# First attention: two half-seen key blocks merged into one, and a new order of the items

## The chip, the cores and the metric

The kernel runs on one core of a Trainium2 chip. The metric is the time of one execution on the device in microseconds (us); lower is better. TensorE (PE) multiplies matrices, VectorE (DVE), ScalarE (ACT) and GpSimd (POOL) work elementwise, SyncE (SP) issues the loads. Each engine runs its own instructions in order; semaphores are all that ties the engines together.

## The reference, cut to what matters

The program computes two transformer layers of different kinds on x of 2 x 512 x 512, in fp32. The change lies in the first layer's attention:

```
q = rope(x @ wq)   # 32 heads of 128         k, v = rope(x @ wk), x @ wv   # 8 heads; 4 q heads share one
scores  = q . k / sqrt(128)
allowed = (j <= i) & (j > i - 128)           # 512 positions
attn    = softmax(where(allowed, scores, -big));   out = (attn @ v) @ wo
```

With positions in blocks of 128, a block of queries sees two blocks of keys: its own where j <= i, and the block before where j > i. In each row the seen columns of the one are just the unseen columns of the other: 128 keys in all. The first query block has no block before.

## The kernel before, in words

For each of 8 key heads and 2 batches (a *half*, `half = 2 * n + b`) the kernel projects K, V and four Q heads, turned so that features lie on partitions, and handles four *slots*, one for each query block `qb` of 128 rows, with its four query heads side by side. Every fp32 product is made of three matmuls of numbers split into a high part (rounded to fp32r) and the low rest, so each operand is written twice: `_hi` by ACT or VectorE, `_lo` by VectorE or POOL (`mm3`, L2032).

A slot goes through these steps. `scores` (PE, L2155) puts the products of four heads with 256 keys into banks 0 and 1. `mask` (DVE, L1538) adds the window to each head's scores by one fused instruction, which also gives the row's maximum. `exps` (ACT, L1070) makes the exponentials of each head and their sums. `normalise` (DVE, L1550) takes reciprocals and multiplies four heads at once, 1024 columns. `transposes` (PE, L2167) turns eight blocks of 128 x 128 into banks 2 and 3. `weights_high` (ACT, L1079) and `weights_low` (DVE, L1560) split them, an instruction per bank. `sum_values` (PE, L2175) multiplies both key blocks with V: six matmuls of 512 columns. `out_high`, `out_low`, `project_out`, `gate_attention` (DVE, L1588) and `add_attention` (POOL, L711) turn the result into an update of x. Slot 0 of a half has one key block, so half of each step.

While the slots of a half run, the next half's projections are made in banks 6 and 7, which alternate: a projection waits until the one before the last has been taken out of its bank (`proj_free`). Q and K leave it by `evacuate` (DVE, L1517; three rope products), `rope_add` (POOL, L693), `rope_high` (ACT) and `rope_low` (POOL, L699); V is copied, transposed back by PE (`Vt`), and split.

The order of all this is written out by hand, in one `kv_head` per engine; each half of the loop has the same items. The loop covers 15 halves; the last half is interleaved with the start of the layer's second part, and the first is preceded by a prologue. `split_weights`, `weights_high0`, `split_wo` and `out_weights_high` prepare the next head's weights, in every other half.

Of the kernel before, what the change touches and what calls it, by code (L numbers as in the profile page):

```python
# [6 lines left out]
F32R = mybir.dt.float32r  # L7
I32 = mybir.dt.int32
# [6 lines left out]
P = 128  # L15
# [51 lines left out]
def adaln_two_layers(nc, a, out):  # L67
# [8 lines left out]
    with ctx:  # L76
# [14 lines left out]
        cT = sb("cT", [P, 2, B, KT])  # L91
        silu_e = sb("silu_e", [P, 2, B, KT])
        silu_d = sb("silu_d", [P, 2, B, KT])
# [29 lines left out]
        v_hi = sb0("v_hi", [P, B, TB, HD], F32R)  # L123
        v_lo = sb0("v_lo", [P, B, TB, HD], F32R)
# [26 lines left out]
        gate_f0 = sb0("gate_f0", [P, B, D])  # L151
        qT_hi, qT_lo = (bq0_hi, bq1_hi), (bq0_lo, bq1_lo)
# [169 lines left out]
        kr_mm, kr_hi_done, kr_split, zeroed = sem("kr_mm"), sem("kr_hi_done"), sem("kr_split"), sem("zeroed")  # L322
# [91 lines left out]
        def _(sp):  # L414
# [44 lines left out]
            sp.dma_start(window[:], a["window_mask"]).then_inc(rope_loaded, 16)  # L459
            load_q(0)  # L460
# [220 lines left out]
        def _(pool):  # L681
# [73 lines left out]
            def kv_head(n, last):  # L755
                for b in range(1 if last else B):
                    half = 2 * n + b
                    split = b == 0 and not last
                    if b == 0:
                        split_wo(n)  # L760
                    if not (isinstance(n, int) and n == 0 and b == 0):
                        add_attention(4 * half - 1, TB * (1 - b) + 3)
# [4 lines left out]
                    rope(half + 1, "Q1", 1 - b)  # L767
                    rope(half + 1, "Q2", 1 - b)
                    add_attention(4 * half, TB * b)
                    rope(half + 1, "Q3", 1 - b)  # L770
                    add_attention(4 * half + 1, TB * b + 1)
                    if split:
                        split_weights(n + 1, (1,))
                    if not last:
                        rope_add(half + 2, "K", b)
                    add_attention(4 * half + 2, TB * b + 2)
                    if not last:
                        rope_low(half + 2, "K", b)
                    if split:
                        split_weights(n + 1, (2,))  # L780
                    if split:
                        split_weights(n + 1, (3, 4, 5))

# [29 lines left out]
            add_attention(4 * LAST - 1, 3)  # L813
            add_attention(4 * LAST, TB)
            add_attention(4 * LAST + 1, TB + 1)
            add_attention(4 * LAST + 2, TB + 2)
# [193 lines left out]
        def _(act):  # L1010
# [55 lines left out]
            def v_high(half, b):  # L1066
                act.wait_ge(proj_done, TURNS * half + TURN["Vt"] + 1)
                act.activation(v_hi[:, b].rearrange("p t d -> p (t d)"), bank[6 + (b + TURN["Vt"]) % 2][:], ACT.Copy).then_inc(v_hi_done, 1)

            def exps(slot, qb):  # L1070
                i = qb % 2
                c = slice(P, 2 * P) if qb == 0 else slice(0, 2 * P)
                act.wait_ge(masked0, slot + 1)
                for h in range(GQ):
                    e = act.activation(probs[:, i, h, c], probs[:, i, h, c], ACT.Exp, bias=nmax[:, i, h:h + 1], scale=-1.0,  # L1075
                                       accum_out=den[:, i, h:h + 1])
# [25 lines left out]
            def kv_head(n, last):  # L1102
                for b in range(1 if last else B):
# [4 lines left out]
                    weights_high(slot, 0)  # L1108
                    out_high(slot)
# [4 lines left out]
                    exps(slot + 1, 1)  # L1114
                    rope_high(half + 1, "Q0", nb)
                    weights_high(slot + 1, 1)
                    v_high(half + 1, nb)
                    exps(slot + 2, 2)
                    rope_high(half + 1, "Q1", nb)
                    out_high(slot + 1)  # L1120
                    weights_high(slot + 2, 2)
                    exps(slot + 3, 3)
                    rope_high(half + 1, "Q2", nb)
                    out_high(slot + 2)
# [1656 lines left out]
```

## Time and profile before

| | |
|---|---|
| median of 3 runs | 2203.28 us (2202.14 to 2205.8) |
| profiled execution, its own time | 2204.66 us |
| its span | 2202.8 us |
| busy over the span: PE, DVE, ACT, POOL | 98%, 77%, 66%, 56% |
| granted TensorE clock, mean | 0.995 |

The first attention takes the stretch from about 60 to 730 us of the span. A busy share is that of an engine's own instructions, waits left out; matmuls overlap, so PE's is no measure of its peak. "Idle before" in a list is the time that an engine waited ahead of the instructions of a group, and the name behind the arrow is what released it. In a list of instructions by time, one that is blocked after it has started shows as longer.

### The profile page before, as it was taken

To read this page: it belongs to the slowest core of one execution; us is meant where nothing else is said; L and a number is where in the kernel's file an instruction comes from. 1 tells how busy PE (TensorE), PEld (TensorE's weight loads), DVE (VectorE), ACT (ScalarE), POOL (GpSimd) and SP (SyncE) were. 2 spreads that over 40 slices of the span, in tenths; PEclk is the share of its full clock that TensorE was granted. 3 is DMA by queue.
4 is the path that set the end of the run, shared out by engine and by line. 5 is a ranking of instruction groups with operands and counts; after the bars stand their busy time and mean duration, and the time that the engine had idled before them with its cause. 6 is when DMAs were issued, how large, how long until landed. Compare 5 with 4: busy or idle time off the path is not lost.

```text
span 2202.8 us, 41666 instructions
## 1 busy us (share of the span) xinstructions
PE 2151.4 (98%) x11084; PEld 1653.8 (75%) x11084; DVE 1700.4 (77%) x3415; ACT 1460.7 (66%) x2868; POOL 1232.4 (56%) x1091
## 2 busy tenths in 40 slices
PE   7999999999999999999999999999999999999988
PEld 5888888888887657777777777777777777777756
DVE  6777777777777668888888888888888877788865
ACT  3444444445444668888888888888888877777742
POOL 5656655665653446666666666666666620455334
PEclk9999999999999999999999999999999999999999
DMA  7011010010004142111111111111111111433341
GB/s 245 20 48 30 19 48 29 19 48 29 19 10 125 40 176 82 43 48 49 46 49 42 49 46 48 42 49 46 49 42 48 47 49 42 124 92 111 87 126 39
DMA packets 125422, 132.20 MB, mean 60 GB/s; under 512 B 33205, under 2 KB 75733, under 8 KB 125348
## 3 DMA queue, kind: packets, MB, share of 16 engines
q1 hardware_dynamic: 121508, 118.70, 18.1%
q0 software_dynamic: 3840, 12.59, 1.9%
q8 instruction: 37, 0.61, 0.1%
q14 instruction: 37, 0.30, 0.0%
HBM read 101.46 MB, written 29.10 MB: 59 GB/s over the span
## 4 chain that ended last, share of the span: by engine, by line
PE 92%; DVE 4%; ACT 1%; SPq 1%; issue 1%; POOL 0%; DMA 0%; DVEq 0%; ACTq 0%; POOLq 0%
PE bank L2464 12%; PE bank L2451 11%; PE bank L2471 11%; PE bank L2036 9%; PE bank L2038 9%; PE bank L2037 9%; PE bank L2492 6%; PE bank L2383 5%; PE bank L2382 5%; PE bank L2381 5%; PE bank L2489 2%; PE bank L2172 2%; DVE rope_b L1535 1%; DVE rope_b L1536 1%; DVE rope_a L1534 1%
## 5 line engine op out<-in xcount | busy, mean ns | idle before, releaser
L1817 DVE TENSOR_REDUCE mcol<-bank 128x1 fp32r<-128x512 f32 x1024 | 693.9, 689 | 221.6 <-PE bank L2451 211.2
L2464 PE MATMUL bank<-q,k 128*128 128x512 f32 x1024 | 418.8, 409 | 0.1
L2451 PE MATMUL bank<-km,q 128*128 128x512 f32 x1024 | 405.7, 397 | 2.9 <-DVE mcol L1817 1.6
L2471 PE MATMUL bank<-q,k 128*128 128x512 f32 x1024 | 406.2, 397 | 0.0
L2451 PEld LDWEIGHTS bank<-km,q 128*128 128x128 f32 x1024 | 316.2, 309 | 52.3 <-DVE mcol L1817 4.2
L1329 ACT ACTIVATE pT<-bank 128x512 f32<-128x512 f32 x512 | 284.5, 600 | 81.6 <-PE bank L2471 77.8
L1329 ACT ACTIVATE x<-bank 128x512 f32<-128x512 f32 x512 | 284.6, 600 | 80.8 <-PE bank L2471 77.0
L2464 PEld LDWEIGHTS bank<-q,k 128*128 128x128 f32 x1024 | 192.2, 188 | 127.0 <-ACT x L1329 44.3
L2471 PEld LDWEIGHTS bank<-q,k 128*128 128x128 f32 x1024 | 192.3, 188 | 32.4
L2383 PE MATMUL bank<-hT_hi,wr_lo 128*128 128x512 f32 x512 | 202.9, 396 | 0.0
L2381 PE MATMUL bank<-hT_hi,wr_hi 128*128 128x512 f32 x512 | 200.7, 392 | 1.6 <-DVE k L1690 1.6
L2382 PE MATMUL bank<-hT_lo,wr_hi 128*128 128x512 f32 x512 | 201.6, 394 | 0.0
L705 POOL TENSOR_TENSOR bq_lo<-rope_a,bq_hi 128x512 fp32r<-128x512 f32 x64 | 105.1, 1644 | 144.1 <-ACT bq_hi L1064 144.1
L849 POOL CAST pH<-x 128x512 f16<-128x512 f32 x96 | 58.7, 612 | 194.0 <-ACT x L1329 194.0
L2036 PE MATMUL bank<-hT_hi,w_hi 128*128 128x512 f32 x376 | 153.5, 408 | 6.9 <-DVE rope_b L1536 6.9
L1075 ACT ACTIVATE probs<-probs,nmax 128x256 f32<-128x256 f32 (+1 forms) x256 | 120.1, 475 | 57.6 <-DVE nmax L1546 57.6
L801 POOL TENSOR_TENSOR wr_lo<-wst,wr_hi 128x512 fp32r<-128x512 f32 x64 | 83.0, 1297 | 129.3 <-DVE wr_hi L1683 129.2
L697 POOL TENSOR_TENSOR rope_a<-rope_a,rope_b 128x512 f32<-128x512 f32 x80 | 111.6, 1394 | 67.3 <-DVE rope_b L1536 67.2
L1082 ACT ACTIVATE pT_hi<-bank 128x512 fp32r<-128x512 f32 x112 | 61.7, 596 | 131.3 <-PE bank L2172 131.3
L2038 PE MATMUL bank<-hT_hi,w_lo 128*128 128x512 f32 x376 | 147.2, 392 | 0.0
L2037 PE MATMUL bank<-hT_lo,w_hi 128*128 128x512 f32 x376 | 146.7, 390 | 0.0
L849 POOL CAST pH<-pT 128x512 f16<-128x512 f32 x96 | 58.5, 610 | 131.0 <-ACT pT L1329 131.0
(348 smaller groups left out, 5045.6 us busy)
## 6 DMA issues: line engine op xcount, KB each, us to landing
wst<-in_L_attn_Wq_rope SPq DMA_DIRECT2D x64, 256.0 KB, 3.0
o_d<-ost SPq DMA_DIRECT2D x504, 32.0 KB, 1.8
st_q<-in_L_attn_wq SPq DMA_DIRECT2D x8, 1024.0 KB, 7.4
st_wo<-in_L_attn_wo SPq DMA_DIRECT2D x8, 1024.0 KB, 5.2
km<-kc_d SPq DMA_DIRECT2D x256, 32.0 KB
q<-qc_d SPq DMA_DIRECT2D x256, 32.0 KB
k<-kc_d SPq DMA_DIRECT2D x256, 32.0 KB
wm<-in_L_wmod SPq DMA_DIRECT2D x6, 1024.0 KB, 9.3
```

What stands on the lines that cost most here:

```text
L1329: act.activation(PT[k % 2][:, s], bank[s % 4][:], ACT.Exp, scale=float((HD1 + ROPE) ** -0.5)).then_inc(exp1, 1)
L1817: dve.tensor_reduce(mcol[:, k % 2, i % 4, i // 4:i // 4 + 1], bank[4 + i % 2][:], AX.X, ALU.max, negate=True)\
L2036: pe.matmul(ps, lh_, rh, start=(i == 0), stop=False)
L2037: pe.matmul(ps, lh_, rl, start=False, stop=False)
L2038: e = pe.matmul(ps, ll, rh, start=False, stop=(i == n - 1))
L2381: pe.matmul(bank[6][:], wr_hi[:, par, kk], hT_hi[:, kk, at], start=(kk == 0), stop=False)
L2382: pe.matmul(bank[6][:], wr_hi[:, par, kk], hT_lo[:, kk, at], start=False, stop=False)
L2383: e = pe.matmul(bank[6][:], wr_lo[:, par, kk], hT_hi[:, kk, at], start=False, stop=(kk == KT - 1))
L2451: pe.matmul(bank[4 + i % 2][:], q2[:, k % 4, h, i % 4:S:4], km[:, b, h], start=True, stop=True).then_inc(max_mm, 1)
L2464: pe.matmul(bank[s % 4][:], k1[:, k % 2, t], q1[:, k % 4, h], start=True, stop=False)
L2471: pe.matmul(bank[s % 4][:], k2[:, k % 2, h, t], q2[:, k % 4, h], start=False, stop=True).then_inc(scores1, 1)
L2492: e = pe.matmul(rows(s), vp[:, k % 2, kb, h], PT[k % 2][:, s], start=(s < 4), stop=(s >= 4))
```

## The change

In slots 1 to 3 the two half-seen blocks are merged into one of 128 columns. `mask` copies the scores of the block before to SBUF, overwrites those of the own block where j <= i by a predicated copy, takes one maximum over the four heads' rows and scales it. `exps`, `normalise`, `transposes` and `weights_high` then handle 128 columns per head. As the merged weights m belong to two value blocks, the sum is made as m times V of the block before, plus (m where own) times the difference of V between the blocks: `weights_low` makes the masked high part, and a new POOL instruction, `own_weights`, the masked low part. `dv_hi` and `dv_lo` hold the difference, made with `Vt` and two new items, `dv_high` (ACT) and `dv_low` (DVE). A 0/1 constant `own` is loaded. Semaphore counts follow (`masked0` goes up by 5 per slot, `pT_split` by 2), and the items of `kv_head` are reordered on all four engines.

```diff
             def exps(slot, qb):
                 i = qb % 2
-                c = slice(P, 2 * P) if qb == 0 else slice(0, 2 * P)
-                act.wait_ge(masked0, slot + 1)
+                c = slice(P, 2 * P) if qb == 0 else slice(0, P)
+                act.wait_ge(masked0, 5 * slot + 5)
...
             def weights_high(slot, qb):
                 act.wait_ge(trans0, slot + 1)
-                for kb in range(1 if qb == 0 else 0, 2):
-                    e = act.activation(pT_hi[:, kb], bank[2 + kb][:], ACT.Copy)
-                e.then_inc(pT_hi_done, 1)
+                act.activation(pT_hi[:, 0], bank[2 + qb % 2][:], ACT.Copy).then_inc(pT_hi_done, 1)
...
+            def own_weights(slot):
+                heads = lambda v: v.rearrange("p (h q) -> p h q", h=GQ)
+                mine = own[:].unsqueeze(1).broadcast_to([P, GQ, P])
+                pool.wait_ge(pT_split, 2 * slot + 1)
+                pool.tensor_tensor(heads(pT_lo[:, 1]), heads(pT_lo[:, 0].bitcast(F32)), mine, ALU.mult).then_inc(pT_split, 1)
...
                 if name == "Vt":
-                    dve.wait_ge(v_hi_done, half + 1)
-                    dve.tensor_tensor(v_lo[:, b]..., ps[:], v_hi[:, b]..., ALU.subtract).then_inc(proj_free, 1)
+                    later = vT[:, 0:3 * P]
+                    dve.wait_ge(v_hi_done, 2 * half + 1)
+                    dve.tensor_tensor(flat(v_lo[:, b]), ps[:, 0:3 * P], flat(v_hi[:, b]).bitcast(F32), ALU.subtract)
+                    dve.tensor_tensor(later, ps[:, P:4 * P], flat(v_hi[:, b]).bitcast(F32), ALU.subtract).then_inc(kv_split, 1)
+                    dve.wait_ge(kv_split, 2 * half + 1)
+                    dve.tensor_tensor(later, later, flat(v_lo[:, b]).bitcast(F32), ALU.subtract).then_inc(proj_free, 1)
...
+            def dv_low(half, b):
+                dve.wait_ge(v_hi_done, 2 * half + 2)
+                dve.tensor_tensor(dv_lo[:]..., vT[:, 0:3 * P], dv_hi[:]..., ALU.subtract).then_inc(kv_split, 1)
...
             def mask(slot, qb):
...
+                block = lambda j, kb: bank[j][:].rearrange("p (h k) -> p h k", h=2)[:, :, kb * P:(kb + 1) * P]
+                seen = window[:, 0:P].bitcast(U32).unsqueeze(1).broadcast_to([P, 2, P])
+                for j in range(2):
+                    dve.tensor_copy(probs[:, i, 2 * j:2 * j + 2, 0:P], block(j, 0)).then_inc(masked0, 1)
+                dve.wait_ge(masked0, 5 * slot + 2)
+                dve.sem_inc(spare, 1)
+                for j in range(2):
+                    e = dve.copy_predicated(probs[:, i, 2 * j:2 * j + 2, 0:P], seen, block(j, 1))
                 e.then_inc(masked0, 1)
+                dve.wait_ge(masked0, 5 * slot + 3)
+                dve.tensor_reduce(nmax[:, i], probs[:, i, :, 0:P], AX.X, ALU.max, negate=True).then_inc(masked0, 1)
+                dve.wait_ge(masked0, 5 * slot + 4)
+                dve.tensor_scalar(nmax[:, i], nmax[:, i], scale, None, ALU.mult).then_inc(masked0, 1)
...
             def weights_low(slot, qb):
                 dve.wait_ge(pT_hi_done, slot + 1)
-                for kb in range(1 if qb == 0 else 0, 2):
-                    e = dve.tensor_tensor(pT_lo[:, kb], bank[2 + kb][:], pT_hi[:, kb].bitcast(F32), ALU.subtract)
-                e.then_inc(pT_split, 1)
+                if qb > 0:
+                    dve.tensor_tensor(heads(pT_hi[:, 1]), heads(bank[2 + qb % 2][:]), own..., ALU.mult)
+                dve.tensor_tensor(pT_lo[:, 0], bank[2 + qb % 2][:], pT_hi[:, 0].bitcast(F32), ALU.subtract)\
+                   .then_inc(pT_split, 2 if qb == 0 else 1)
```

The order of a half's items on VectorE and TensorE (`s` the half's first slot, primes the next half):

```
DVE before: gate(s-1) mask(s+1) weights_low(s) Q0' Q1' out_low(s) normalise(s+1) mask(s+2) weights_low(s+1) Vt'
            gate(s) normalise(s+2) out_low(s+1) Q2' mask(s+3) weights_low(s+2) normalise(s+3) Q3' out_low(s+2)
            gate(s+1) weights_low(s+3) gate(s+2) K'' mask(s+4) out_low(s+3) V'' normalise(s+4)
DVE after:  gate(s-1) mask(s+1) weights_low(s) Q0' normalise(s+1) Q1' mask(s+2) out_low(s) weights_low(s+1) Vt'
            gate(s) normalise(s+2) Q2' out_low(s+1) weights_low(s+2) mask(s+3) Q3' gate(s+1) normalise(s+3)
            out_low(s+2) K'' weights_low(s+3) mask(s+4) out_low(s+3) gate(s+2) dv_low' V'' normalise(s+4)
PE before:  scores(s+1) T(s) Q0' sum(s) Q1' Vt' scores(s+2) Q2' T(s+1) out(s) sum(s+1) scores(s+3) T(s+2) Q3'
            out(s+1) sum(s+2) T(s+3) K'' out(s+2) sum(s+3) scores(s+4) V'' out(s+3)
PE after:   scores(s+1) T(s) Q0' sum(s) Q1' scores(s+2) Vt' T(s+1) Q2' out(s) scores(s+3) sum(s+1) T(s+2) Q3'
            out(s+1) sum(s+2) K'' T(s+3) out(s+2) scores(s+4) sum(s+3) V'' out(s+3)
```

On POOL, `own_weights(s+1)` comes behind Q1's rope items, `own_weights(s+2)` behind Q2's, `own_weights(s+3)` ahead of K's; `add_attention(s)` moves ahead of Q2's, and the `add_attention` of the slot before moves ahead of `split_wo`. On ACT, `weights_high(s+2)` moves ahead of `out_high(s+1)`, and two of the next head's weight splits move ahead of `exps(s+2)`.

## Rows read from the trace of the kernel before

**Rows 1.** Stretches: us, busy PE PEld DVE ACT POOL (x), clock, DMA share, GB/s.
```profile
342.90:384.97 42.07, 41.58 (x222) 35.43 (x222) 31.28 (x73) 19.29 (x54) 25.59 (x20) 1.00 0.12 37
```
**Rows 2.** Waits, 130 to 690 us: us in total, times, longest.
```profile
PE bank L2036 <- DVE rope_b L1536: 6.3, 13, 0.5
```
**Rows 3.** Chain of waits, one half: start, us, what.
```profile
357.51 0.44 PE bank L2172 x4
...
365.64 0.69 DVE rope_b L1536
...
369.46 0.87 PE bank L2172 x8
```
**Rows 4.** Instructions by time, TensorE, same half: start, us.
```profile
355.91 0.28 PE L2036 MATMUL bank<-kT_hi,bq_hi 128*128 128x256 f32 x1
...
360.53 0.39 PE L2036 MATMUL bank<-pT_hi,v_hi 128*128 128x512 f32 x1
...
361.21 0.39 PE L2036 MATMUL bank<-hT_hi,w_hi 128*128 128x512 f32 x1
...
363.94 0.60 PE L2145 MATMUL bank<-ident,vT 128*128 128x128 f32 x4
...
365.68 0.28 PE L2038 MATMUL bank<-kT_hi,bq_lo 128*128 128x256 f32 x1
366.45 0.49 PE L2036 MATMUL bank<-hT_hi,w_hi 128*128 128x512 f32 x1 [0.49 <-DVE rope_b L1536]
366.78 0.39 PE L2037 MATMUL bank<-hT_lo,w_hi 128*128 128x512 f32 x1
```
**Rows 5.** Instructions by time, VectorE, same half.
```profile
357.70 0.42 DVE L1546 CUSTOM_DVE_ANT_0 probs<-bank,window 128x256 f32<-128x256 f32 x1 [0.90 <-PE bank L2038]
...
358.06 0.42 DVE L1546 CUSTOM_DVE_ANT_0 probs<-bank,window 128x256 f32<-128x256 f32 x1
...
358.40 0.42 DVE L1546 CUSTOM_DVE_ANT_0 probs<-bank,window 128x256 f32<-128x256 f32 x1
...
366.35 0.69 DVE L1568 TENSOR_TENSOR oT_lo<-bank,oT_hi 128x512 fp32r<-128x512 f32 x1
366.96 0.17 DVE L1554 RECIPROCAL rden<-den 128x4 f32<-128x4 f32 x1
367.16 1.61 DVE L1557 TENSOR_TENSOR probs<-probs,rden 128x1024 f32<-128x1024 f32 x1
```
**Rows 6.** Groups by line and shape, whole span; one line's own instructions (L1481).
```profile
L1817 DVE TENSOR_REDUCE mcol<-bank 128x1 fp32r<-128x512 f32 x1024 | 693.9, 689 | 221.6 <-PE bank L2451 211.2
L1528 DVE COPY vT<-bank 128x512 f32<-128x512 f32 x16 | 11.0, 690 | 14.9 <-PE bank L2038 14.9
L1546 DVE CUSTOM_DVE_ANT_0 probs<-bank,window 128x128 f32<-128x128 f32 x64 | 14.8, 287 | 3.5 <-PE bank L2038 2.2 <-issue 0.6
L1481 DVE TENSOR_SCALAR var_eps<-mean_var x8: 169/170/540, 10.9 to 2147.3; 128x4 f32<-128x4 f32 x8
```
**Rows 7.** Instructions by time, VectorE and POOL: products alone and beside POOL.
```profile
354.21 0.69 DVE L1557 TENSOR_TENSOR probs<-probs,rden 128x512 f32<-128x512 f32 x1
374.14 1.22 DVE L1557 TENSOR_TENSOR probs<-probs,rden 128x1024 f32<-128x1024 f32 x1
396.27 1.69 DVE L1557 TENSOR_TENSOR probs<-probs,rden 128x512 f32<-128x512 f32 x1
366.40 1.29 POOL L697 TENSOR_TENSOR rope_a<-rope_a,rope_b 128x512 f32<-128x512 f32 x1 [0.17 <-DVE rope_b L1536]
374.49 2.02 POOL L705 TENSOR_TENSOR bq_lo<-rope_a,bq_hi 128x512 fp32r<-128x512 f32 x1 [6.80 <-ACT bq_hi L1064]
396.12 1.29 POOL L705 TENSOR_TENSOR kT_lo<-rope_a,kT_hi 128x512 fp32r<-128x512 f32 x1 [0.74 <-ACT kT_hi L1064]
```
**Rows 8.** Chain of waits, prologue.
```profile
40.20 0.69 DVE rope_a L1534
...
51.30 1.27 POOL rope_a L697
```

More of the change, by code:

```diff
@@ L151, in adaln_two_layers @@
         gate_f0 = sb0("gate_f0", [P, B, D])
+        with ExitStack() as first:
+            sbs = sbuf_in(first)
+            cT = sbs("cT", [P, 2, B, KT])
+            silu_e = sbs("silu_e", [P, 2, B, KT])
+            silu_d = sbs("silu_d", [P, 2, B, KT])
+        dv_lo = sb0("dv_lo", [P, TB - 1, HD], F32R)
         qT_hi, qT_lo = (bq0_hi, bq1_hi), (bq0_lo, bq1_lo)
@@ L773, in kv_head @@
                         split_weights(n + 1, (1,))
+                    own_weights(4 * half + 3)
                     if not last:
@@ L782, in kv_head @@
                         split_weights(n + 1, (3, 4, 5))
+                    if not last:
+                        rope_low(half + 2, "K", b)
             kv_head(0, False)
@@ L1135, in kv_head @@
                         weights_high0(n + 1, 5)
+                    out_high(slot + 2)
+                    rope_high(half + 1, "Q3", nb)
+                    weights_high(slot + 3, 3)
                     if not last:
                         rope_high(half + 2, "K", b)
+                    out_high(slot + 3)
+                    dv_high(half + 1, nb)
+                    exps(slot + 4, 0)
             def merged_turned(t):
@@ L1527, in evacuate @@
                 if name == "V":
+                    wait(dve, kv_split, 2 * half)
                     dve.tensor_copy(vT[:], ps[:]).then_inc(proj_free, 1)
@@ L2157, in scores @@
                     pe.wait_ge(rope_split, 5 * half + 5)
-                wait(pe, masked0, slot)
+                wait(pe, masked0, 5 * slot if qb == 1 else 5 * slot - 2)
                 c = slice(P, 2 * P) if qb == 0 else slice(0, 2 * P)
@@ L2179, in sum_values @@
                 wait(pe, oT_split, slot)
-                mm3(bank[4][:], [(v_hi[:, b, qb - 1 + kb], v_lo[:, b, qb - 1 + kb], pT_hi[:, kb], pT_lo[:, kb])
-                                 for kb in range(1 if qb == 0 else 0, 2)], pv0)
+                at = max(qb - 1, 0)
+                pe.matmul(bank[4][:], v_hi[:, b, at], pT_hi[:, 0], start=True, stop=False)
+                pe.matmul(bank[4][:], v_hi[:, b, at], pT_lo[:, 0], start=False, stop=False)
+                e = pe.matmul(bank[4][:], v_lo[:, b, at], pT_hi[:, 0], start=False, stop=(qb == 0))
+                if qb > 0:
+                    pe.wait_ge(pT_split, 2 * slot + 2)
+                    pe.matmul(bank[4][:], dv_hi[:, at], pT_hi[:, 1], start=False, stop=False)
+                    pe.matmul(bank[4][:], dv_hi[:, at], pT_lo[:, 1], start=False, stop=False)
+                    e = pe.matmul(bank[4][:], dv_lo[:, at], pT_hi[:, 1], start=False, stop=True)
+                e.then_inc(pv0, 1)
             def project_out(slot, n):
@@ L2239, in kv_head @@
                     project(half + 1, "Q1", nb, n + b)
+                    scores(slot + 2, half, b, 2)
                     project(half + 1, "Vt", nb, n + b)
-                    scores(slot + 2, half, b, 2)
+                    transposes(slot + 1, 1)
                     project(half + 1, "Q2", nb, n + b)
-                    transposes(slot + 1, 1)
                     project_out(slot, n)
+                    scores(slot + 3, half, b, 3)
                     sum_values(slot + 1, half, b, 1)
-                    scores(slot + 3, half, b, 3)
                     transposes(slot + 2, 2)
@@ L2250, in kv_head @@
                     sum_values(slot + 2, half, b, 2)
-                    transposes(slot + 3, 3)
                     if not last:
                         project(half + 2, "K", b, n + 1)
+                    transposes(slot + 3, 3)
                     project_out(slot + 2, n)
+                    scores(slot + 4, half + 1, nb, 0)
                     sum_values(slot + 3, half, b, 3)
+                    if not last:
+                        project(half + 2, "V", b, n + 1)
                     if isinstance(n, int) and n == 0 and b == 0:
                         pe.wait_ge(gate_ready, 1)
-                    scores(slot + 4, half + 1, nb, 0)
-                    if not last:
-                        project(half + 2, "V", b, n + 1)
                     project_out(slot + 3, n)
```

119 lines of the change are left out of this document (66 added, 53 removed).

## The prediction, made before the changed kernel was run

> **What bounds the kernel now.** I read the table of busy time by stretch first, with the granted clock beside it: the middle of the first attention, cut at its own period [rows 1]. A half (one key head, one batch) takes 42.07 us; in it TensorE is busy 41.6 us at the full clock (1.00), VectorE 31.3, ACT 19.3, POOL 25.6. So TensorE sets the pace, and VectorE has some 10 us of idle time. Then the list of waits of the stage [rows 2]: what TensorE itself waits for is a rope product of VectorE, 6.3 us in 13 waits. The chain of waits of one half shows where that sits: after the second set of scores the third query projection waits for the rope products of the second, because both use one PSUM bank [rows 3]. The order of TensorE's instructions says what such a wait costs [rows 4]: the last scores matmul starts at 365.68 and the next would start 0.12 later, at 365.80; it starts at 366.45, and its successor follows after 0.33 instead of the usual 0.23. So 0.65 + 0.10 = 0.75 us per half. All starts below are counted from the half's first scores, 355.91 [rows 4]. Without that wait a half would take 42.07 - 0.75 = 41.32 us.
>
> **What goes from TensorE.** Four transposes take 0.44 us of the chain, eight take 0.87 [rows 3]. In three slots of four, eight become four: 3 x 0.435 = 1.31 us per half. The matmuls of the weights with the values stay six (three on the block before, three on the difference). So 41.32 - 1.31 = 40.01 us is the floor of a half, 2.06 below now; there are 15 full halves, so at most 31 us.
>
> **What VectorE gets.** It is the engine that has to follow, so each piece is priced.
> - The mask now is four fused instructions of 256 columns, 0.34 us apart (358.06 to 358.40), so 4 x 0.34 = 1.37 us [rows 5]. In its place: two copies of 256 columns from PSUM, two predicated copies, one reduce of 512, one multiplication of four numbers, with three waits for its own results between. A 512-column read of PSUM takes 0.69 [rows 6] and the 256-column one 0.42, with the next 0.34 later [rows 5]: a pair ends after 0.34 + 0.42, and 0.04 passes at a wait for one's own result, as between reciprocal (0.17) and product [rows 5]. Copies 0.80, predicated copies 0.80, reduce 0.69 + 0.04 (a reduce of 512 columns takes 0.69, from PSUM [rows 6]; from SBUF I take the same), multiplication 0.1: 2.43 us. No row shows a predicated copy. From below it is bounded by the 128-column instruction, 0.29, from above by the 512-column one, 0.69 [rows 6]; I take 0.42, that of equal width. The mask so lies between 2.2 and 3.0 us.
> - The product with the reciprocals is 512 columns instead of 1024: 0.69 instead of 1.22 when undisturbed [rows 7]. The low weights stay two instructions of 0.61. The values' low part becomes three dependent instructions (0.47 + 0.56 + 0.03 + 0.56 = 1.6 in place of 0.61) and the difference's low part adds 0.5.
> - Per half: 3 x (2.43 - 1.37) - 3 x 0.5 + 1.0 + 0.5 = +3.2 us. That fits the 10 us of idle time as a sum; whether it fits in the order is the question.
>
> **The port.** A product of two SBUF tensors waits for POOL. The 512-column one takes 0.69 alone and 1.69 when POOL has begun an instruction 0.15 us earlier, ending 0.55 after POOL's; and POOL takes 2.02 in place of 1.29 when the product came first [rows 7]. Right behind rope products POOL wins: it starts 0.08 after their end (366.32 to 366.40), the product 0.2 behind the reciprocal that lies between [rows 3, 5, 7]. The four-number multiplication takes 0.17 and once 0.54 [rows 6], so it too seems to wait.
> The Trainium skill's page "SBUF — State Buffer", section "Who interferes with whom", says the same of products and of a multiplication on SBUF data (whoever begins first blocks the other for its whole instruction), and adds that a reduce never takes part; the trace has no reduce from SBUF beside POOL. By that rule the sum stays as below; were the reduce to wait as well, each mask could grow by up to a POOL instruction, 1.29, which is more of the slower rival.
>
> **The order, followed through one half.** TensorE's pieces are read from [rows 4]: a projection of twelve matmuls 2.73 us (361.21 to 363.94), also the output's; three matmuls of the values 0.68 (360.53 to 361.21), so six 1.37; scores 1.42 with the transposes of V ahead of them 1.86 (363.94 to 365.80); four transposes 0.44. VectorE's: rope products three times 0.70, a two-input instruction on PSUM 0.61 to the next [rows 5].
> 1. Scores end, mask from 1.79 (where it starts now [rows 4, 5]) to 4.22; low weights of the slot before end 4.91, TensorE gets them at 5.04 (0.13 later, as from 366.32 to 366.45 [rows 3, 4]). It wants them at 4.62: late by 0.42.
> 2. Rope products of Q0 4.83 to 6.94. The product of the slot, now ahead of Q1's, waits for POOL's rope sum (7.02 to 8.31) and ends at 8.86. Q1's projection, itself moved by step 1, is ready at 8.85, so the port costs nothing here. Rope products of Q1 to 10.95; Q2 starts at 11.08. Without waits it would be 10.34 (Vt and the transposes are ahead of it). Cost of steps 1 and 2 together 0.74 + 0.10 = 0.85 us. So the old wait stays, since everything from the mask on is one VectorE chain.
> 3. Next mask to 13.4, and the low output, now behind it, to 14.1; the output projection, due 2.83 after Q2's start at 13.91, starts at 14.23: 0.32 + 0.10 = 0.42 us.
> 4. TensorE: output projection to 17.06, scores to 18.48, six matmuls to 19.85, where it wants the next product. VectorE's low weights and the values' part end by 17.4, the gate (behind the output projection) at 18.0, the product behind `own_weights` at about 19.3: in time. `own_weights` of this slot runs on POOL from about 17.2 to 18.5 and is wanted at 19.2.
> 5. Rope products of Q2 to 21.5, low output at 22.3 (it waits for ACT), low weights 23.5, mask 26.0 plus 0.3 for the small multiplication behind `own_weights`, rope products of Q3 28.35, gate 28.96, product behind POOL's rope sum 30.25. TensorE wants it at 19.85 + 0.44 + 2.73 + 2.73 + 1.37 + 2.73 = 29.85, gets it at 30.38: 0.53 + 0.10 = 0.6 us (rounded).
> 6. The rest of the half: key rope, low weights by 35, first mask, difference's low part and `own_weights` come before their readers.
>
> The waits come to 0.85 + 0.42 + 0.60 = 1.87 us, so a half takes 40.01 + 1.87 = 41.88: 0.19 us less than now, 15 x 0.19 = 2.8 us.
> POOL's three `own_weights` are 3 x 1.29 [rows 7], on an engine with 16 us idle per half; behind them queue the adds of x and the rope sums, which have microseconds. ACT loses a copy and half of the exponentials' columns per slot, in an engine idle for more than half of the time [rows 1]. The DMA of the new constant is 64 KB behind loads that TensorE doesn't wait for.
>
> **Before and after the loop.** In the prologue the chain runs through VectorE from 40.20 to 51.2 and then through POOL [rows 8]. The longer values' part (+1.0) and the difference's low part (+0.6) stand in it: +1.6 us. In the last half three sets of transposes go (-1.3), and the waits for VectorE's longer masks take some 0.5 back: -0.8.
>
> **Sum.** The profiled execution took 2204.66 us (span 2202.8). -2.8 + 1.6 - 0.8 = -2.0: 2202.7 us. It lies 1.4 above the median of the runs shown, 2203.28; from the median the forecast is 2201.3, say 2201. About 0.2% (4.4 us) is what a measurement can tell from no change.
>
> **The rivals.**
> - *VectorE keeps up* (25%). If the mask costs 2.0 us instead of 2.43, steps 1 to 3 lose 0.9 us and step 5 about 0.45 more, to about 0.5 of waits: 15 x -1.5 = -23, about 2181; with no wait at all 2203 - 31 + 1 = 2173. For it: 10 us idle per half, and new waits sit at a few tenths. Against: every step of the new mask waits for the one before.
> - *The predicated copy costs double* (20%; the other side). At 0.69 each, the mask is 0.54 longer; it stands three times in the chain that TensorE waits for, and the first time it counts more because Q1 moves too, 3.25 x 0.54 = 1.75 per half: 15 x 1.75 - 2 = +24, about 2227. It decides from about 0.06 us more per copy on. For it: nothing shows this instruction. Against: equal width costs equal time in all others [rows 5, 6].
> - *`own_weights` comes late* (10%). The second three matmuls wait for POOL, which serves a rope sum and a rope remainder first. In slot 2 it has 0.2 us to spare by my count; late by 0.6 in two of three slots (2 x 0.5 + 0.2 lost) it is +1.2 per half, 15 x 1.2 - 2 = +16, about 2219.
> - *The change saves no TensorE time* because transposes hide behind weight loads: 2203 + 1 plus the waits, above 2215; the 0.44 to 0.87 step of rows 3 speaks against it, I give it nothing of its own.
>
> **How the numbers follow.** The forecast 45%, with its own range 2194 to 2209 (a tenth of a microsecond per mask is 0.33 per half, 5 us in all); the rivals 25, 20 and 10. The range of 8 in 10 is 2180 to 2224: it takes in most of the first and a good part of the second. Faster by over 0.2%: 25 + 12 = 37%. Within 0.2%: 28%. Slower: 30 + 5 = 35%.
>
> **What would show it.** After: transposes 256 instead of 448; four rows of 0.44 us in the chain; mask steps 0.42, 0.42, 0.42, 0.42, 0.69 and under 0.2, 2.4 us together; a half of 41.9 us, with TensorE's idle time at Q2 (0.75), at the first output projection (0.3) and before the transposes of slot 3 (0.5), released by VectorE; VectorE's idle time per half down from 10 to some 7 us. It is wrong if a predicated copy is not 0.42, if TensorE's waits name POOL, or if a half is outside 41.4 to 42.4.

## The result, and the profile after

The changed kernel takes 2256.07 us (median of 4 runs, 2255.61 to 2260.36) against 2204.54 us of the kernel before on the same chip (2202.14 to 2205.89): a ratio of 1.0239, 95% interval 1.0222 to 1.0257. The profiled execution took 2256.01 us. The forecast was 2201, with a range of 2180 to 2224: the change costs 51.5 us where 2 us of gain were expected.

The first rows of the page: the span, and each engine's busy time and instructions.
```profile
span 2254.2 us, 41585 instructions
PE 2169.3 (96%) x10892; PEld 1643.4 (73%) x10892; DVE 1794.3 (80%) x3367; ACT 1422.4 (63%) x2836; POOL 1288.2 (57%) x1139
```
Three halves of the changed kernel, the view of [rows 1]: us, busy PE PEld DVE ACT POOL, clock, DMA share, GB/s. The first two belong to batch 0, the third to batch 1.
```profile
242.01:286.99 44.98, 41.71 (x211) 33.92 (x209) 38.44 (x69) 19.77 (x54) 30.57 (x21) 1.00 0.07 23
330.11:377.92 47.81, 44.56 (x210) 36.04 (x209) 38.44 (x69) 19.66 (x54) 30.62 (x21) 0.93 0.06 22
377.92:421.07 43.15, 41.77 (x210) 33.95 (x209) 36.91 (x69) 14.74 (x47) 28.16 (x22) 1.00 0.11 36
```
A half took 42.07 us whatever its batch [rows 1]. Now a half of batch 1 takes 43.1 us (the first 42.9) and one of batch 0 45.0 to 48.3, so the last half starts 44.0 us later than before (736.8 against 692.8 us): 1.5 us from ahead of the loop, 42.5 in its 15 halves (673.8 against 631.3). Look at TensorE's busy time: 41.7 us in the first and the third, but 44.56 in the second, for the same instructions, at a clock of 0.93.

The list of waits, 130 to 690 us, as in [rows 2]:
```profile
ACT probs L1100 <- DVE nmax L1600: 92.0, 37, 4.3
...
PE bank L2236 <- DVE pT_lo L1616: 24.6, 12, 2.9
```
The old wait for the rope products is gone from it. TensorE waits for `weights_low` ahead of the first values of each half, up to 2.9 us (3.4 in the first half, which this window leaves out). VectorE by time there shows why (start, us):
```profile
332.77 0.79 DVE L1595 COPY_PREDICATED probs<-window,bank 128x256 f32<-128x256 uint32 x2
333.59 0.69 DVE L1598 TENSOR_REDUCE nmax<-probs 128x4 f32<-128x512 f32 x1
334.31 2.72 DVE L1600 TENSOR_SCALAR nmax<-nmax 128x4 f32<-128x4 f32 x1
336.95 0.68 DVE L1616 TENSOR_TENSOR pT_lo<-bank,pT_hi 128x512 fp32r<-128x512 f32 x1
```
and GpSimd beside it:
```profile
332.44 4.57 POOL L698 TENSOR_TENSOR wo_lo<-st_wo,wo_hi 128x2048 fp32r<-128x2048 f32 x1
```
The multiplication of four numbers begins at 334.31 and ends at 337.03; GpSimd's `wo_lo` ends at 337.01. The Trainium skill's page "SBUF — State Buffer", section "Who interferes with whom", counts a `tensor_scalar` from on-chip memory to on-chip memory among the instructions that can contend with GpSimd, and says that whichever of the two engines issues second is fully blocked until the other's instruction is over. The trace agrees, with 2.72 us in place of 0.17. It also shows that semaphores are not all that ties the engines together: none stands between these two instructions. In batch-1 halves GpSimd has only instructions of 1.3 us there, and the multiplication takes 1.20 us. All forms of the line together (smallest, median, largest, ns):
```profile
L1600 DVE TENSOR_SCALAR nmax<-nmax x48: 169/170/3368, 67.2 to 754.9; 128x4 f32<-128x4 f32 x48
```
TensorE behind two of these waits, in a half that kept its clock and in one that lost it (from the timeline of its own instructions):
```profile
249.75 0.47 PE L2236 MATMUL bank<-pT_hi,v_hi 128*128 128x512 f32 x1 [2.91 <-DVE pT_lo L1616]
250.06 0.40 PE L2237 MATMUL bank<-pT_lo,v_hi 128*128 128x512 f32 x1
250.29 0.39 PE L2238 MATMUL bank<-pT_hi,v_lo 128*128 128x512 f32 x1
...
337.87 0.76 PE L2236 MATMUL bank<-pT_hi,v_hi 128*128 128x512 f32 x1 [2.91 <-DVE pT_lo L1616]
338.43 0.63 PE L2237 MATMUL bank<-pT_lo,v_hi 128*128 128x512 f32 x1
338.86 0.63 PE L2238 MATMUL bank<-pT_hi,v_lo 128*128 128x512 f32 x1
...
343.55 0.63 PE L2092 MATMUL bank<-hT_lo,w_hi 128*128 128x512 f32 x1
343.98 0.44 PE L2093 MATMUL bank<-hT_hi,w_lo 128*128 128x512 f32 x1
```
The wait is 2.91 us both times. After the first the matmuls follow each other every 0.23 us, the 2.4 GHz level. After the second they come every 0.43 us up to 343.98, the 1.2 GHz level: 13 matmuls take 5.55 us instead of 3.0, so 2.5 us are lost behind a wait of 2.9. The half does not win them back: its first output projection starts 20.0 us after its start, against 17.2 in the half that kept the clock. Two batch-0 halves of eight (45.0 us) kept it. The others lost it, for 3 to 6 us: the first five of those are 1.3 to 2.8 us longer, 8.8 together.

The product with the reciprocals (L1608), the pieces of the mask and one piece of the values' low part (L1553), as groups of the whole span:
```profile
L1608 DVE TENSOR_TENSOR probs<-probs,rden 128x512 f32<-128x512 f32 x64 | 73.2, 1144 | 2.2
L1595 DVE COPY_PREDICATED probs<-window,bank 128x256 f32<-128x256 uint32 x96 | 37.6, 445 | 7.1 <-DVE probs L1591 3.4
L1600 DVE TENSOR_SCALAR nmax<-nmax 128x4 f32<-128x4 f32 x48 | 36.2, 754 | 1.7
L1591 DVE COPY probs<-bank 128x256 f32<-128x256 f32 x96 | 36.1, 418 | 15.8 <-PE bank L2093 15.3
L1598 DVE TENSOR_REDUCE nmax<-probs 128x4 f32<-128x512 f32 x48 | 32.9, 686 | 1.6
L1553 DVE TENSOR_TENSOR vT<-vT,v_lo 128x384 f32<-128x384 f32 x15 | 18.6, 1239 | 0.5
```
Copy, predicated copy and reduce are as forecast (0.42, 0.45, 0.69 us). The mean of 0.754 us for the multiplication is no typical value: its median is 0.17, and the long ones all stand in slot 1. L1553, another product of two on-chip tensors, took 1.24 us where the forecast had 0.56.

### The profile page after: what moved, and what is told of

The parts are those of the page before. It is cut to its first block, busy times and chain, and to the rows that moved or that the text cites. A ratio compares the mean times of both kernels' runs of the same rounds, so it can differ in the third digit from the quotient of the medians.

```text
span 2254.2 us, 41585 instructions
## 1 busy us (share of the span) xinstructions
PE 2169.3 (96%) x10892; PEld 1643.4 (73%) x10892; DVE 1794.3 (80%) x3367; ACT 1422.4 (63%) x2836; POOL 1288.2 (57%) x1139
## 4 chain that ended last, share of the span: by engine, by line
PE 87%; DVE 7%; issue 3%; ACT 1%; POOL 1%; SPq 1%; DMA 0%; DVEq 0%; ACTq 0%; POOLq 0%
PE bank L2527 12%; PE bank L2514 11%; PE bank L2534 10%; PE bank L2091 7%; PE bank L2093 7%; PE bank L2092 7%; PE bank L2555 6%; PE bank L2446 5%; PE bank L2444 5%; PE bank L2445 5%; PE bank L2552 2%; PE bank L2236 1%; PE bank L2227 1%; DVE probs L1591 1%; DVE nmax L1598 1%
## 5 line engine op out<-in xcount | busy, mean ns | idle before, releaser
L1100 ACT ACTIVATE probs<-probs,nmax 128x128 f32<-128x128 f32 x256 | 99.6, 390 | 120.1 <-DVE nmax L1600 116.1
L704 POOL TENSOR_TENSOR rope_a<-rope_a,rope_b 128x512 f32<-128x512 f32 x80 | 103.5, 1294 | 102.8 <-DVE rope_b L1566 102.8
L1106 ACT ACTIVATE pT_hi<-bank 128x512 fp32r<-128x512 f32 x64 | 38.3, 598 | 163.8 <-PE bank L2227 163.8
L712 POOL TENSOR_TENSOR bq_lo<-rope_a,bq_hi 128x512 fp32r<-128x512 f32 x64 | 83.1, 1300 | 83.6 <-ACT bq_hi L1084 83.6
```

## The experiments

All timed against the kernel before, run on the same chip (2205.2 to 2206.5 us). Where "one run" stands there is a single execution, and no interval. A half's length is the time between the first scores of slot 1 in two successive halves, read from TensorE's timeline.

**e1_tables and e1b_recip: the multiplication taken away, or something that cannot be blocked in its place.** The factor 1/sqrt(128) goes into the rope tables (its root in each; `exps` then scales by 1), and the reduce signals in its place. The second kernel has, beyond that, a reciprocal of the four maxima that nobody reads.
```
-    scale = float(HD) ** -0.5
+    scale = 1.0
-    dve.tensor_reduce(nmax...).then_inc(masked0, 1)
-    dve.wait_ge(masked0, 5 * slot + 4)
-    dve.tensor_scalar(nmax[:, i], nmax[:, i], scale, None, ALU.mult).then_inc(masked0, 1)
+    dve.tensor_reduce(nmax...).then_inc(masked0, 2)
+    "rope_cos": cos * HD ** -0.25      (rope_sin likewise)
```

> The changed kernel, with the factor 128^-0.5 of the scores put into the rope tables of q and k (128^-0.25 each), so that the small multiplication of four maxima in the mask is gone; everything else as in the changed kernel. Theory (the small multiplication waits for the SBUF port while POOL works: 2.7 us in every half of batch 0 behind the 4.6 us split of wo, 1.2 in the others): TensorE's wait before the first value matmuls falls from 2.9 and 1.2 us to 0.2 to 0.5 in all halves, TensorE's clock no longer falls in the loop, a half takes 42.0 to 42.4 us instead of 43.15 and 45.0 to 48.3, the time is 2212 to 2218 us. Rival (the chain of five dependent steps in the mask is simply long, the instruction's own 0.17 us is all that goes): 3 x 0.2 x 15 = 9 us, about 2247.

> As the kernel with the factor in the tables, but in place of the multiplication stands a reciprocal of the same four numbers into a spare tile: same place, same wait, same 0.17 us, an instruction that never waited for POOL in the traces so far. Port theory: 0.17 us in all 48 places, and the time within 5 us of the kernel without the instruction (2214 to 2222). Rival (a fifth dependent step costs): within 10 us of the changed kernel, 2246 or more.

Measured: e1_tables 2213.5 us (5 runs; ratio to before 1.0041, 1.0026 to 1.0055), halves 41.6 to 42.0 us (the last of the loop 42.6), TensorE idle 0.25 us ahead of the first values in batch 0 and hardly at all in batch 1. The multiplication of four numbers, three times in each half, was worth 42.6 us (43.3 with each kernel taken against the kernel before of its own chip). e1b_recip 2212.7 us (one run), halves 41.9 to 42.5 (the last 44.2). Its line:
```profile
L1601 DVE RECIPROCAL spare<-nmax x48: 177/178/179, 66.3 to 715.8; 128x4 f32<-128x4 f32 x48
```
A reciprocal of the same size, same place and same operand was never held. So it is the kind of instruction, not its place behind the reduce. Yet e1_tables stays 8 us over the kernel before, though its loop (628.5 us) is as fast as forecast.

**e2_pieces: `wo_lo` of the changed kernel in four instructions of 512 columns.**
```
-    pool.tensor_tensor(wo_lo[:], st_wo[:], wo_hi[:]...).then_inc(wo_split, 1)
+    for h in range(GQ):
+        e = pool.tensor_tensor(wo_lo[:, h], st_wo[:, h], wo_hi[:, h]...)
+    e.then_inc(wo_split, 1)
```

> The changed kernel with POOL's 2048-column split of wo cut into four instructions of 512 columns (4 x 1.3 us). Port theory: the small multiplication waits for one piece at most, so its 2.7 us in halves of batch 0 become 1.3 or less, TensorE's wait 2.9 becomes 1.4 or less, the clock stays up, these halves take 43.2 to 43.6 us instead of 45.0 to 48.3: 2230 to 2238 us. If POOL's pieces kept the port between them (no hand-over), nothing changes: 2256. If the wait has nothing to do with POOL: 2256.

Measured: 2228.0 us (one run), waits of 0.9 us in batch 0 and 1.2 in batch 1, halves 42.9 to 43.2 us (the first 42.1, the last 44.5), clock 0.993 instead of 0.989. The multiplication is held for 0.7 us in batch 0, where it was 2.7. A shorter GpSimd instruction makes a shorter block, and waits of about 1 us left the clock alone. The result is a little below what was expected.

**e3_old_order: merged blocks, order of items as before.** 

> The merged blocks as in the changed kernel, but the items of the loop in the order of the kernel before on all four engines (the new items put in at the first place where their inputs are there). Port theory: the small multiplication stands in the same place against the split of wo, so the 2.7 us wait stays in half of the halves; time within 12 us of 2256. Rival (the new order is what costs): the time comes back to 2200 to 2215.

Measured: 2391.5 us (one run). Both expected times missed by over 120 us; the multiplication was held as in the changed kernel (2.6 us in batch 0, 3.7 in the first half; 1.1 to 1.3 in batch 1). TensorE's list of waits, 130 to 690 us:
```profile
PE bank L2241 <- POOL pT_lo L723: 63.0, 22, 4.0
PE bank L2236 <- DVE pT_lo L1616: 19.8, 10, 2.8
```
So most of TensorE's waiting there is for `own_weights` on GpSimd. The new order is worth 135 us to the merged version; it is no cause of the loss.

**b2_small: the same kind of instruction, alone, in the kernel before.**
```
+    if qb > 0:
+        dve.tensor_scalar(spare4[:], ident[:, 0:GQ], 0.5, None, ALU.mult)
```

> The kernel before plus one multiplication of four numbers per partition that nobody reads (a tile of its own from the first four columns of ident), on VectorE behind each mask of query blocks 1 to 3. Theory 1 (a small tensor_scalar waits for the end of a GpSimd operation on the tensors): wherever it falls inside wo_lo (4.6 us) or w_lo it takes 1 to 4 us, elsewhere 0.17 us, though it depends on nothing; at least 8 of the 48 are longer than 1 us and the total rises by 3 to 25 us. Theory 2 (it was long in the changed kernel only because it depended on the reduction just ahead, or had its own result as operand): 0.17 to 0.2 us in all 48, total within 3 us of the kernel before.

Measured: 2246.7 us (one run), 41 us slower, more than either theory gave. VectorE, then GpSimd:
```profile
422.93 3.62 DVE L1551 TENSOR_SCALAR spare<-ident 128x4 f32<-128x4 f32 x1
426.46 0.68 DVE L1566 TENSOR_TENSOR pT_lo<-bank,pT_hi 128x512 fp32r<-128x512 f32 x1
```
```profile
421.95 4.57 POOL L692 TENSOR_TENSOR wo_lo<-st_wo,wo_hi 128x2048 fp32r<-128x2048 f32 x1 [2.90 <-ACT wo_hi L1101]
```
It depends on nothing and nobody reads it, and it still waits for the end of `wo_lo` (426.52). Batch-0 halves took 45.4 to 47.5 us. So this one instruction reproduces most of the loss without merged blocks or a new order. Not all of the 41 us are its own: its tile of 16 bytes also moved the other tiles, by 32 bytes, and b1_layout below shows what a move can cost (5.5 us in the loop, 11 in all).

**e4_late_max: the changed kernel with reduce and multiplication of slot 1 behind `weights_low`.**
```
     mask(slot + 1, 1)              # copies and predicated copies only
     weights_low(slot, 0)
+    maximum(slot + 1, 1)           # reduce, multiplication
```

> The changed kernel as it is, with its multiplication of the four maxima, but in slot 1 of each half the reduction and the multiplication stand behind weights_low(slot 0). Theory 1 (the long multiplication costs because weights_low and so the first value matmuls are queued behind it): the multiplication still takes about 2 to 2.7 us in batch-0 halves and 1.2 us in batch-1 halves, the TensorE no longer waits 2.9 and 1.2 us before the first value matmuls, the clock does not fall in the loop, and the time comes to 2212 to 2225 us. Theory 2 (whatever is held on VectorE for 2.7 us is paid in full, since exps(slot 1) and the rope products of Q0 come after it): the wait shows up before the second projection or the transposition instead, total 2240 us or more.

Measured: 2245.8 us (one run): the pessimistic theory. Halves 42.4 and 44.1 to 46.2 us (the last 48.0); the multiplication held for 2.3 us in batch 0 and 0.75 in batch 1. TensorE, 130 to 690 us:
```profile
PE bank L2098 <- DVE rope_b L1566: 12.9, 12, 1.4
PE bank L2234 <- DVE probs L1613: 5.8, 10, 0.9
```
Moved behind one reader, the same block hits the next two, as VectorE works through one chain. And the clock falls behind two shorter waits, 2 us apart (two batch-0 halves, of 44.1 and 44.2 us, had the same two waits and kept it):
```profile
428.50 0.66 PE L2234 MATMUL bank<-ident,probs 128*128 128x128 f32 x4 [0.81 <-DVE probs L1613]
430.50 0.49 PE L2098 MATMUL bank<-hT_hi,w_hi 128*128 128x512 f32 x1 [1.35 <-DVE rope_b L1566]
...
431.70 0.63 PE L2099 MATMUL bank<-hT_lo,w_hi 128*128 128x512 f32 x1
432.13 0.63 PE L2100 MATMUL bank<-hT_hi,w_lo 128*128 128x512 f32 x1
```

**b1_layout: the kernel before with the tiles moved, and nothing else.** The change moves cT, silu_e and silu_d (192 bytes) from the front of the memory to its end, and with them every large tile of the first attention.
```
-    cT = sb(...); silu_e = sb(...); silu_d = sb(...)      # ahead of rowsum
+    with ExitStack() as first:                            # behind gate_f0
+        cT = sbs(...); silu_e = sbs(...); silu_d = sbs(...)
```

> The kernel before with one part of the change alone: the tiles cT, silu_e and silu_d stand behind gate_f0 instead of in front of rowsum, so every later tensor of the second attention lies 192 bytes lower in each partition; no instruction is added or removed. In all four kernels profiled with the change, the second attention, where TensorE is busy all the time, took 749.1 to 751.9 us between the 100th and the 400th matmul hT_hi x wr_hi, against 748.0 before. Theory 1 (addresses): this stretch takes 750 to 751 us here too and the total rises by 4 to 8 us. Theory 2 (it is the scatter of executions, or it comes from something else of the change): 748.0 +- 0.5 us and a total within 2 us of the kernel before.

Measured: 2216.7 us (4 runs; ratio 1.0051, 1.0034 to 1.0068): 11 us slower without one instruction changed. Halves 42.47 us, matmuls 100 to 400 of `hT_hi x wr_hi` 750.6 us. In a projection of twelve matmuls, first of it and first instruction behind it:
```profile
366.92 0.39 PE L2038 MATMUL bank<-hT_hi,w_hi 128*128 128x512 f32 x1
...
369.72 0.60 PE L2147 MATMUL bank<-ident,vT 128*128 128x128 f32 x4
```
2.80 us, against 361.21 to 363.94 = 2.73 before [rows 4]. Six projections make 0.4 us per half, the whole of the difference between halves. That is theory 1, with more than it asked for: the loop is 5.5 us longer (636.8 us), and the stretch of the second attention from its first `wr` matmul to its last 6.1 us (1305.5 against 1299.4).

**e6_tables_late: e1_tables with the late maximum.** 

> The changed kernel with the factor in the rope tables (no multiplication of the four maxima) and, in slot 1 of each half, the reduction moved behind weights_low(slot 0): VectorE does the copies, the predicated copies, weights_low, then the maximum. With the factor in the tables alone the TensorE waited 0.25 us before the first value matmuls and a half took 41.6 to 42.0 us. Theory 1 (the queue of VectorE sets that wait): it is gone, the reduction's 0.69 us now delays exps(slot 1), which has over 5 us until its transposition; halves 41.4 to 41.8 us, start of the last half 3 to 5 us earlier than with the tables alone, total 2207 to 2212 us. Theory 2 (the next wait, VectorE's rope products, takes its place): halves unchanged within 0.1 us, total 2211 to 2216 us.

Measured: 2210.1 us (10 runs; 1.0021, 1.0011 to 1.0030). The wait ahead of the values is gone, and rope_b took its place (5.6 us in 13 waits); halves 41.8 and 41.9. The total lies in the range of theory 1, but the halves are within 0.1 us of e1_tables and the next wait took the place of the old one: theory 2.

**e7_aligned, b3_pad128, e8_after_aligned: which places are good.** e7 is e6_tables_late and e8 the changed kernel, both with nmax and den behind dv_lo, which brings the large tiles 64 bytes lower; b3 is the kernel before with an unused tile of 128 bytes ahead of rowsum. The edit of e7 and e8:
```
-    nmax = sb("nmax", [P, 2, GQ]); den = sb("den", [P, 2, GQ])
     dv_lo = sb0("dv_lo", [P, TB - 1, HD], F32R)
+    nmax = sb0("nmax", [P, 2, GQ]); den = sb0("den", [P, 2, GQ])
```

> The kernel with the factor in the tables and the late maximum in slot 1, with nmax and den moved behind dv_lo, so that w_hi, w_lo and all other large tensors lie 64 bytes lower and again at a multiple of 128 bytes from the first tensor, as in the kernel before (in the changed kernel they lie 64 bytes off one). Moving the three small tiles alone, without any change of an instruction, had cost the kernel before 11 us (2216.72 against 2205.66), with 0.2333 us instead of 0.2281 from one projection matmul to the next. Theory 1 (the start of the matmuls' operands against 128 bytes sets it): spacing 0.228 us, halves 41.4 to 41.6 us, stretch of the second attention 748 us, total 2197 to 2202 us, faster than the kernel before. Theory 2 (only the exact place of before is good, or the relation to something else): spacing 0.233, halves 41.8 to 42.0, total 2208 to 2212 us.

> The kernel before with an unused tile of 128 bytes in front of rowsum: everything behind it lies 128 bytes higher, still at multiples of 128 bytes. Theory 1 (128 bytes): spacing 0.228 us, halves 42.07 us, total within 2 us of the kernel before. Theory 2 (any other place than that of before costs, or a multiple of 256 or 512 bytes is wanted): spacing 0.233 us, halves 42.47 us, total 2214 to 2218 us.

> The changed kernel with all its instructions, nmax and den moved behind dv_lo as above. It prices the tiles' places within the change. Theory 1 (128 bytes): 2243 to 2247 us, that is 9 to 13 us of the change's 51 us come from the places of the tiles and 38 to 42 from the multiplication; batch-1 halves 42.7 to 42.8 us instead of 43.14. Theory 2: 2254 to 2258 us, halves as in the changed kernel.

Measured: b3_pad128 2215.4 us (4 runs; 1.0045, 1.0030 to 1.0060), a projection in 2.80 us, halves 42.4: against the theory, 128 bytes are not enough. e7_aligned 2208.0 us (11 runs; 1.0007, 0.9998 to 1.0016), e8_after_aligned 2249.7 us (2 runs, 2246.5 and 2252.9), both with projections of 2.72 us where the clock was full. In e8 a half of batch 1 takes 43.0 us, 0.1 less than in the changed kernel. For e7 the spacing is that of theory 1, the total that of theory 2; of e8's two runs one lies in the range of theory 1, the other between the two. e7_aligned:
```profile
365.39 0.39 PE L2096 MATMUL bank<-hT_hi,w_hi 128*128 128x512 f32 x1
...
368.11 0.28 PE L2096 MATMUL bank<-kT_hi,bq_hi 128*128 128x256 f32 x1
```
```profile
PE bank L2096 <- DVE rope_b L1566: 6.7, 13, 0.6
PE bank L2232 <- DVE probs L1611: 2.8, 2, 2.5
PE bank L2096 <- DVE oT_lo L1624: 1.3, 6, 0.2
```
VectorE's product in slot 1, beside GpSimd's rope sum, comes late for the first of them:
```profile
367.25 1.67 DVE L1611 TENSOR_TENSOR probs<-probs,rden 128x512 f32<-128x512 f32 x1
```

**e9_no_collision: e7_aligned with GpSimd kept off the product in slot 1.**
```
     split_wo(n)                      # heads 0 and 1 only
+    pool.wait_ge(probs0, 4 * half + 2)
     rope_add(half + 1, "Q0", 1 - b)
+    if b == 0: split_wo_rest(n)      # heads 2 and 3
```

> The kernel e7_aligned (factor in the tables, late maximum in slot 1, tiles at the places modulo 256 bytes of before) with GpSimd's work in slot 1 arranged around VectorE's product of weights and reciprocals: GpSimd begins the addition of Q0's rope only when that product is done (one wait more), and wo_lo is made in two halves, one ahead of it and one behind. In e7_aligned the projection matmuls were 0.005 us faster each than without the alignment (0.36 us of 72 per half), but the halves stayed at 41.75 and 41.87 us: TensorE waits 0.47 to 0.57 us for Q1's rope_b ahead of the projection of Q2, and VectorE comes late there because its product took 1.67 us beside GpSimd's addition (0.99 us in slot 2, where GpSimd was idle). Theory 1 (this collision took the gain): the product takes 1.0 to 1.1 us, the wait for rope_b falls to 0 to 0.1 us, halves 41.3 to 41.5 us, total 2200 to 2204 us, faster than the kernel before. Theory 2 (VectorE's queue is late for other reasons, or the next wait replaces it): halves 41.7 to 41.9 us, total 2206 to 2210 us.

Measured: 2201.05 us (median of 12 runs, one of which took 5392.5 us; 2200.94 without it, 0.9975 of the kernel before, 0.9966 to 0.9985). This version beats both kernels, by 5 us and by 55. The half that answers to [rows 1], then VectorE's product:
```profile
352.14:393.48 41.34, 41.23 (x211) 34.03 (x210) 34.26 (x66) 14.68 (x47) 28.10 (x22) 1.00 0.12 38
```
```profile
359.31 0.69 DVE L1617 TENSOR_TENSOR probs<-probs,rden 128x512 f32<-128x512 f32 x1
```
The product took 1.67 us at this place in e7 beside GpSimd's rope sum, and takes 0.69 alone; TensorE's wait for rope_b has left the list. Halves are 41.33 (batch 1) and 41.59 us (batch 0, where the product of slot 2 is now held, for 1.74 us instead of 0.99). The total is that of theory 1, and so are the halves of batch 1; it had the others 0.1 us shorter.

TensorE in that half, at the transposes of slot 1:
```profile
362.04 0.60 PE L2238 MATMUL bank<-ident,probs 128*128 128x128 f32 x4
362.68 0.49 PE L2102 MATMUL bank<-hT_hi,w_hi 128*128 128x512 f32 x1
```
From the start of the transposes to the next matmul it is 0.64 us here, and 0.36 and 0.53 in slots 2 and 3. The eight transposes of the kernel before took 0.79 each time (369.30 to 370.09). So the merged blocks give TensorE 0.84 us per half at these places, where 1.31 was forecast.

## Why the prediction was wrong

- **The step that failed is the mask's sum in "What VectorE gets", with its "multiplication 0.1", and "The port", which should have mended it.** The port paragraph had the rule, the row of the held product [rows 7] and the one multiplication that had taken 0.54 [rows 6], and it concluded that this instruction "too seems to wait". Step 5 then charged 0.3 us for it in slot 3, where it takes 0.17. Step 1 charged nothing in slot 1, where GpSimd's `split_wo` and its work on the weights run beside it. Measured there: 2.7 us in batch 0 (3.4 in the first half), 1.2 in batch 1. None of its rivals had this wait. The 4.6 us of `split_wo`, from 2.3 us into each batch-0 half on (332.44 against a start at 330.11), were never laid beside the mask, which stands at the same place.
- **The cost was the wait and the clock.** By e1_tables the multiplication costs 42.6 us in all, and 45.3 of the loop (673.8 against 628.5 us). In the loop the later start of the first values accounts for (7.74 - 5.08) x 8 = 21 us in batch 0 and (6.03 - 4.90) x 7 = 8 in batch 1. By the halves that kept the clock against those that lost it, 9 us are TensorE at 1.2 GHz in five halves, and up to 3 more in the last half of the loop. The rest, 4 to 5 us, is 0.1 to 0.2 us more at each of the first output projection and the transposes of slot 3. The clock had no place in the forecast; nothing in the kernel before had a wait of this length in the loop.
- **The places of the tiles were no step at all.** They cost 11 us in the kernel before (b1_layout), some 6 in the changed one (3 to 10 by e8's two runs) and 2 without the multiplication (e6_tables_late against e7_aligned), where waits took the gain.
- **The sum.** Taken away one after the other, each against the kernel before of its own chip: 51.5 us, 8.3 without the multiplication, 4.5 with the late maximum too (a help that the change does not have), 2.8 with the tiles back on the multiple (-0.4 to +3.5 by the interval). The -2.0 of the forecast stands in none of these totals.
- **Steps that held.** Transposes: 256. Predicated copy 0.445 us against 0.42; the rival that had it double is out. Prologue: from the first projection matmul to the first scores of the loop 39.9 us instead of 38.6, +1.3 against +1.6. (Counted from the start of the span it is +1.5, but there the first projection starts anywhere from 20 to 25 us in these kernels.)
- **A step that came out right by luck is the half of 41.88.** With the two unforeseen costs removed (e7_aligned), the loop takes 628.6 us against 631.3, -2.7 where the forecast had -2.8, and halves of 41.75 and 41.87. But the waits in it are smaller than counted: at the projection of Q2 0.7 us (0.85 forecast for steps 1 and 2), at the first output 0.2 (0.42), at slot 3 0.2 (0.60), 1.1 together instead of 1.87. So the floor under them, 40.01, was too low by some 0.7 us. e9 shows it too: its half without a listed wait, with three starts that come 0.15 to 0.2 us late (at two outputs and at slot 3), still takes 41.33. Half a microsecond is the transposes (0.84 us saved, not 1.31); the rest was not traced. Two errors of opposite sign made the agreement.
- **Leverage per mask.** "A tenth of a microsecond per mask is 0.33 per half" was high, by one run: e1b_recip adds 0.2 us to each mask and 0.45 us to a half, 0.23 per tenth (its spare tile also moves the large tiles, by 32 bytes).
- **The last half** was forecast at -0.8 and came to +0.4 in the changed kernel. From its start to the first `wr` matmul the changed kernel took 92.8 us, e1_tables 93.0, e9 92.1, the kernel before 92.4.
- **`own_weights` comes late** (10%) did not happen in the new order: no wait of TensorE there names GpSimd. In the old order it is the main one (e3).

Left open: why a multiple of 256 bytes is wanted, and whether it is w or its distance from hT that counts (all variants moved the one and not the other); what decided which waits of 2.9 us lost the clock; and the tail from the last `wr` matmul to the end, 117 to 122 us from kernel to kernel without an order that the experiments explain.

## What to carry to other kernels

Price a small instruction by what runs on GpSimd beside it, not by its size: if it is a `tensor_scalar` that reads and writes on-chip memory, its worst case is the longest GpSimd instruction that can lie there, and everything behind it on VectorE pays. Fold constants into tables, or use a form that is not held, and keep long GpSimd instructions away from VectorE's critical chain. When a change adds or moves tiles, compare the starts of the matmuls' operands before and after, and run the old kernel once with the new places.

## What the runs showed that was not expected

- A `tensor_scalar` of four numbers is held for up to 3.4 us (4.4 in b2_small) by GpSimd, a reciprocal of the same four numbers never (0.177 to 0.179 us, 48 times), a reduce from on-chip memory never (0.685 to 0.690 us, 48 times in e2_pieces and in the changed kernel, there in the midst of `wo_lo`).
- TensorE's clock falls to 1.2 GHz for 3 to 6 us behind some waits of 2.9 us and not behind others of the same length (changed kernel); behind single waits of 0.9 to 1.2 us it stayed (e2_pieces, halves of 42.9 to 43.2 us), behind two of 0.8 and 1.35 us in a row it fell for 3 us in some halves and stayed in others (e4_late_max).
- Moving tiles by 64, 128 or 32 bytes off a multiple of 256 turns a projection of twelve matmuls from 2.72 to 2.80 us, and by 64 or 128 bytes the kernel of 2205 us into one of 2215 to 2217, at equal instructions and clock.
- The chain of waits does not name GpSimd where it holds VectorE through the port: TensorE's wait is put down to the VectorE instruction behind, and only the duration of the multiplication (2.72 for 0.17 us) gives it away.
